# Head attention: where the next head's right-operand loads stand in SP's queue, and where a head's reciprocals stand on VectorE

## What is computed

```python
b, t, c = x.shape                       # 4, 1024, 128
nh, hs = 16, 8
y = x.reshape(b, t, nh, hs).transpose(0, 2, 1, 3)
scores = jnp.einsum('bhtk,bhsk->bhts', y, y) / math.sqrt(hs)
attn = jax.nn.softmax(scores, axis=-1)
o = jnp.einsum('bhts,bsc->bhtc', attn, x)
return o.transpose(0, 2, 1, 3).reshape(b, t, nh * c) @ weight
```

## Time and profile before

| | us |
|---|---|
| median of 3 runs | 2703.54 |
| lowest and highest run | 2698.01, 2705.41 |
| the profiled execution | 2697.12 |
| span of the profiled execution, first to last instruction | 2695.3 |
| TensorE busy in the span | 2519.3 (93%) |
| VectorE busy | 2166.5 (80%) |
| ScalarE busy | 1826.3 (68%) |
| GpSimd busy | 1213.5 (45%) |
| mean granted TensorE clock, of full speed | 0.973 |

### The profile page before, as it was taken

The page is one execution under the profiler, slowest core; times in us unless marked ns, Lnnn a source line. Parts: engine busy times, 40 slices in busy tenths (PEclk is TensorE's granted clock), DMA queues, the critical chain, the costliest instruction groups (busy, mean ns, idle before and its releaser), DMA issues. The chain is left out here.

```text
span 2695.3 us, 34921 instructions
## 1 busy us (share of the span) xinstructions
PE 2519.3 (93%) x11075; PEld 1901.4 (71%) x11075; DVE 2166.5 (80%) x2872; ACT 1826.3 (68%) x3038; POOL 1213.5 (45%) x1258
## 2 busy tenths in 40 slices
PE   7899999996999999999999998899999999788888
PEld 4788888874666666666666665688888886567656
DVE  6677777776999999999989996777777776578665
ACT  4455555556888888888888985455555555657676
POOL 3566666664223323233223222366666664154401
PEclk9999999998999999999999998999999999888899
DMA  4566666645333333333333331566666660000001
GB/s 111 115 143 141 137 137 138 145 97 167 100 107 101 101 109 102 103 104 100 104 102 101 101 104 34 116 137 142 142 145 144 142 142 9 24 24 9 9 3 37
DMA packets 107384, 271.46 MB, mean 101 GB/s; under 512 B 30784, under 2 KB 35648, under 8 KB 107072
## 3 DMA queue, kind: packets, MB, share of 16 engines
q1 hardware_dynamic: 82192, 235.42, 35.1%
q0 software_dynamic: 24576, 33.62, 4.5%
q10 hardware_dynamic: 432, 0.20, 0.0%
HBM read 258.35 MB, written 10.76 MB: 100 GB/s over the span
## 5 line engine op out<-in xcount | busy, mean ns | idle before, releaser
L684 POOL TENSOR_TENSOR moe_experts_lo<-moe_experts_hidden,moe_experts_hi 128x512 fp32r<-128x512 f32 x512 | 661.0, 1291 | 341.6 <-ACT moe_experts_hi L622 341.5
L962 DVE TENSOR_TENSOR heads_e_lo<-heads_e,heads_e_hi 128x2048 fp32r<-128x2048 f32 x256 | 585.5, 2287 | 54.9 <-ACT heads_e_hi L910 52.3
L629 ACT ACTIVATE psum<-psum 128x512 f32<-128x512 f32 x512 | 298.0, 582 | 478.9 <-PE psum L90 478.9
L797 POOL DMA_DIRECT2D heads_left<-heads_parts x512 | 296.1, 600 | 678.5 <-PE psum L851 613.8
L903 ACT ACTIVATE heads_e<-psum 128x1024 f32<-128x1024 f32 x512 | 520.1, 1023 | 104.0 <-PE psum L851 104.0
L656 DVE TENSOR_TENSOR moe_experts_weighted<-moe_spread,psum 128x512 f32<-128x512 f32 x512 | 350.8, 685 | 189.8 <-PE psum L90 185.8
L88 PE MATMUL psum<-heads_e_hi,heads_v_lo 128*128 128x512 f32 x1024 | 425.3, 415 | 1.4 <-DVE heads_u L929 1.4
L88 PE MATMUL psum<-moe_n_hi,moe_w_lo 128*128 128x512 f32 x1024 | 400.8, 391 | 5.8 <-PEq L54 5.7
L89 PE MATMUL psum<-heads_e_lo,heads_v_hi 128*128 128x512 f32 x1024 | 402.5, 393 | 0.0
L90 PE MATMUL psum<-heads_e_hi,heads_v_hi 128*128 128x512 f32 x1024 | 401.2, 392 | 0.0
L89 PE MATMUL psum<-moe_n_lo,moe_w_hi 128*128 128x512 f32 x1024 | 399.8, 390 | 0.0
(11 more groups left out here) (403 smaller groups left out, 4057.2 us busy)
## 6 DMA issues: line engine op xcount, KB each, us to landing
moe_spread<-moe_mask SPq DMA_DIRECT2D x128, 1024.0 KB, 10.1
heads_right<-heads_parts SPq DMA_DIRECT2D x512, 64.0 KB
heads_left<-heads_parts POOLq DMA_DIRECT2D x512, 64.0 KB, 2.7
heads_scale<-heads_inverse_copy SPq DMA_DIRECT2D x64, 512.0 KB, 3.6
moe_experts_raw<-in_gate SPq DMA_DIRECT2D x16, 256.0 KB, 11.6
moe_experts_raw<-in_up SPq DMA_DIRECT2D x16, 256.0 KB, 11.6
moe_experts_raw<-in_down SPq DMA_DIRECT2D x16, 256.0 KB, 11.6
heads_parts<-heads_e_hi SPq DMA_DIRECT2D x16, 256.0 KB, 3.2
```

What stands on the lines that cost most here:

```text
L629: act.activation(psum[:, GATE + p % 2, :], psum[:, GATE + p % 2, :], ACT.Silu).then_inc(silu_ready, 1)
L684: pool.tensor_tensor(lo[:, p, :], hidden[:, p % 2, :], f(hi[:, p, :]), ALU.subtract).then_inc(low_ready, 1)
L797: eng.dma_start(f(tile[row:row + 2 * HEAD, h % 2, :]), parts_dram[dims, order:order + 2, at]).then_inc(loaded[h % 2], 16)
L962: dve.tensor_tensor(e_lo[:, s:s + 2, :], e[:, s % 4:s % 4 + 2, :], f(e_hi[:, s:s + 2, :]), ALU.subtract).then_inc(low, 1)
```

## The change

On SP the eight right loads of head h+2, with their wait for the scores of head h, stand first in the body of the loop, ahead of the wait for the reciprocals of head h. On VectorE `invert(h)` stands in step s = 6 of head h itself, directly behind the low parts of that step, in place of `invert(h-1)` in step s = 0 of head h; the last one is then in the loop too. Nothing is added or taken away.

```diff
                 for h in range(COUNT):
+                    if h + 2 < COUNT:
+                        sp.wait_ge(scores_done, (h + 1) * TILES)
+                        load_head(sp, right, (0, 1), h + 2, right_loaded)
                     sp.wait_ge(inverse_ready, h + 1)
                     after(sp, scale_loaded[h % 2], 16 * (h // 2))
                     for b in range(P // 32):
...
                     sp.dma_start(scale[:, h % 2, :], inverse_dram[h % 2:h % 2 + 1, :].to_broadcast([P, T])
                                  ).then_inc(scale_loaded[h % 2], 16)
-                    if h + 2 < COUNT:
-                        sp.wait_ge(scores_done, (h + 1) * TILES)
-                        load_head(sp, right, (0, 1), h + 2, right_loaded)
...
                     dve.tensor_copy(e_hi[:, s, :], e[:, s % 4, :]).then_inc(dve_high, 1)
-                    if s == 0 and h >= 1:
-                        invert(h - 1)
                     if s == 4 and h >= 1:
                         scale_sums(h - 1)
...
                                       ALU.subtract).then_inc(low, 1)
+                    if s == TILES - 2:
+                        invert(h)
                     if s == TILES - 2 and h >= 1:
                         u_lows(h - 1)
...
-                invert(COUNT - 1)
                 scale_sums(COUNT - 1)
```

## The result

The changed kernel takes 2667.46 us (median of 4 runs, 2660.37 to 2672.28) against 2704.26 before (4 runs): a ratio of 0.9866, 95% interval 0.9838 to 0.9895, so 36.8 us faster. The profiled execution took 2670.02 us, with a span of 2668.2. The profiled one of before took 2697.12, so the two profiles differ by 27.1 us; the sum was 27.3.

A forecast was written before the change was run, and what follows sets the result against it. TensorE was taken to pause before first scores in some 30 of 60 heads, waiting for late right loads. Pauses 25.3, head 2 1.9, end 1.1, less 1.0, give 27.3 us: from 2703.5 to 2676.2, range 2668 to 2690.

The forecast's parts named there:

- the sum: Whole kernel: 25.3 + 1.9 + 1.1 - 1.0 = 27.3 us gained, 24 to 29 by the bounds.
- Pauses before s = 0: Head attention: TensorE's pauses before a head's first scores, from late right loads, all go; 24.6 to 25.9, taken as 25.3 us.
- part 1: SP's queue: right loads go first, with about 9.5 us to spare, ending all pauses before first scores; 25.3 us.
- part 2: VectorE: reciprocals 1.73 us earlier, removing nearly all of 5.4 us of waits for the scale; nothing counted for these.
- Head 2: Head attention, head 2: its last step takes 4.80 us in place of 6.73; 1.9 us gained.
- The end: End of the head attention: last reciprocals begin 1.1 us earlier, the last `scale_sums` waiting for its scale load; 1.1 us gained.
- What stays: Head attention: `add_batch` in three heads and an occasional slow scale load may still cost time; 1.0 us kept, bounds 0 and 3.
- Stores right behind loads cost nothing, by the direct row: SP's queue: first store to scale load stays 2.17 us, as measured for stores after GpSimd's left loads; no cost taken.
- the upper bound: SP's queue: stores can't count as landed before the right loads; scale load 6.5 us behind the head's start, landed at 10.1.
- room for the scale: Head attention: scale lands 8.1 to 8.7 us behind the head's start, `scale_sums` begins at 10.4; some 1.7 us to spare.
- The slower rival: Head attention: scale load becomes the late one if queueing adds over 3.1 us; at 3.5 us, 61 us cost, 2737; chance 0.05.
- VectorE takes over: Head attention: VectorE's waits don't shrink, its floor is 15.33 us a head; only 10 us gained, 2693; chance 0.07.

The follow-up runs named there:

- e1: Changed kernel with only the right loads moved first on SP, reciprocals where they stood before: 2671.02 us (6 runs), ratio 0.9903 to the kernel before.
- e2: Changed kernel with only the reciprocals moved earlier, right loads still behind the scale load: 2673.35 us (6 runs), ratio 0.9908 to the kernel before.
- e7: e2 with a 1 KB copy and a wait for it ahead of the right loads: 2804.55 us (4 runs), ratio 1.0389 to the kernel before.
- e4: Changed kernel with GpSimd's left loads waiting for two more steps' scores: 2669.33 us.
- e5: Changed kernel with one 1 KB copy and a wait for it ahead of each scale load: 2698.91 us (9 runs), ratio 1.0001 to the kernel before.
- e0: Changed kernel once more, no edit: 2670.90 us (4 runs) against 2698.32 for the kernel before, ratio 0.9899.
- e6: Changed kernel with two 1 KB copies, each waited for, ahead of each scale load: 2795.18 us (4 runs), ratio 1.036 to the kernel before.

## Why the prediction was right, and where it wasn't

- **Pauses before s = 0, 25.3 us**: right. 24.2 us in the profile; e1 and e2 show that either part does it, e7 that the right loads are the cause. The prediction credited all of it to part 1; part 2 alone is worth as much.
- **Head 2, 1.9 us**: 1.8 (15.14 us in place of 16.96).
- **The end, 1.1 us**: 0.9, and TensorE became its last wait. The row at 1641.19 that the prediction took for the last weighted rows is `add_head`, which stands right behind them; they ended at about the same time, so only some 0.9 of the 1.1 us could be had.
- **What stays, 1.0 us**: 1.7 by its own measure. The pauses of before were counted against 15.02 a head; 902.89 less 60 x 15.02 is 1.7 us. Three heads with `add_batch` cost 0.2 each, one slow scale load 0.7.
- **"Stores right behind loads cost nothing, by the direct row"**: wrong. The first store to the scale load takes 4.14 us, not 2.17. The direct row had left loads, on the other queue, and was taken for right loads ahead on SP's own queue with left loads beside them; e4 and the packets show that this makes the difference. The step that failed is the choice of that row over the upper bound. The bound itself, stores held until the right loads have landed and the scale load at 6.5 us behind the head's start, had the mechanism that the packets show, and it held (6.35 in the median). So the 2 us cost no time, but the margin was small: of 1.7 us of room for the scale 0.4 is left (6.35 + 3.6 against 10.4), and e5, 1.4 us later, is as slow as the kernel before.
- **The slower rival** was priced rightly (TensorE bears 0.91 us of lateness, 0.85 foretold; beyond it, one for one), and its mechanism appeared with 2.0 us where it needed 3.1. It deserved more than the 0.05 it got.
- **VectorE takes over**: no. It runs at 15.03 us a head with 14.34 of work (860.39 / 60), and its waits for ScalarE shrank from 48.0 to 21.1 us without anything done for it.
- **The sum and the median**: 27.3 foretold, 27.1 between the profiles and 27.4 in e0; the first comparison of medians says 36.8. The step that failed is the one from the profile to the median and its range: the sum was set against a median of three runs, with 2668 as the low end, while executions of either kernel alone spread over 12 us with the granted clock of the layers behind (13 us between e1's and e2's profiles). The low end should have allowed for that spread in both medians.

More readings of the traces agree with the prediction's upper bound, by which the stores don't count as landed before the right loads have: it is shown for these runs, not as a rule. In the five runs with all eight right loads ahead of the stores (the changed kernel, e1, e4, e5, e6) the last store packet ends behind the last right packet in every head from 3 to 61, by 0.06 us at the least. From the last store packet to the scale load it is 1.46 us in the changed kernel, where right loads end just before, against 0.34 in e4, where they are done 1.2 us earlier. And the copy of e7 comes back 0.19 us after the load ahead of it.

What stays open is why left and right loads together run slower. The packets show that each takes longer (0.27 us against 0.16), not whether that lies with the DMA engines or the memory.

## What to carry to other kernels

When a load is the last thing a stage waits for, look at what it stands behind in its queue: here it waited for a chain (reciprocals, stores, their landing, a scale load) that it had nothing to do with, and 1.8 us earlier by either way was enough. Then look at what the moved load runs beside: its new place put 512 KB of loads in front of a small round trip, with as much again beside them on another queue, and used up most of the room of the next wait. Only a row with the same traffic, in the same queue, could have priced that. And set a gain of 1% against several interleaved runs of both kernels, not one median of three.

## What the runs showed of the hardware that was not expected

- Four small stores with their round trip took 2.17 us behind eight 64 KB loads alone, on their own queue (e4, issued 0.8 us before) or on the other, and 4.14 us with both (changed kernel). With both, a packet of the right loads took 0.27 us in place of 0.16, and the stores' last packet ended 0.07 us after the last right packet.
- A 1 KB copy came back in about 1.9 us where no large load was issued right ahead of it on its queue (e5). Directly behind a 512 KB load it took 3.4 us, and was back 0.19 us after that load had landed (e7).
- The granted clock of the stretch was 0.95 in e7, where TensorE paused for up to 5.0 us at a time before the first scores, and 0.98 in e6; in the kernel before, with pauses of up to 1.9 us, it was 1.00.
